# A decoder layer's recurrent scan on VectorE: outer product by heads, corrections by broadcast, fewer waits; with row groups in the LoRA matmuls and a new order in the product-key stage

## What is computed

```python
def step(state, rkv):
    r_t, k_t, v_t = rkv
    pred = jnp.einsum('bhij,bhj->bhi', state, k_t)
    err = pred - v_t
    state = dec * state - et * (err[..., :, None] * k_t[..., None, :])
    n = jnp.maximum(jnp.sqrt(jnp.sum(state * state, axis=(-2, -1), keepdims=True)), 1e-08)
    state = state * jnp.where(n > max_norm, max_norm / n, 1.0)
    wkv = jnp.einsum('bhij,bhj->bhi', state, r_t)
```

## Time and profile before

| | us |
|---|---|
| three runs, median (lowest to highest) | 6758.13 (6751.82 to 6759.17) |
| the profiled execution, its own time | 6756.8 |
| its span in the trace | 6755.0 |
| mean granted TensorE clock, share of full speed | 0.949 |
| PE busy in the span | 5962.8 |
| DVE busy | 5530.5 |
| ACT busy | 3576.0 |
| POOL busy | 3730.7 |

### The profile page before, as it was taken

The page is one execution under the profiler, slowest core; times in us unless marked ns, Lnnn a source line. Parts: engine busy times, 40 slices in busy tenths (PEclk is TensorE's granted clock), DMA queues, the critical chain, the costliest instruction groups (busy, mean ns, idle before and its releaser), DMA issues. The chain is left out here.

```text
span 6755.0 us, 179966 instructions
## 1 busy us (share of the span) xinstructions
PE 5962.8 (88%) x76324; PEld 4338.5 (64%) x76324; DVE 5530.5 (82%) x10471; ACT 3576.0 (53%) x8048; POOL 3730.7 (55%) x1761
## 2 busy tenths in 40 slices
PE   7566666799998899999999999999788789999999
PEld 5466665677777755555555555555566578888888
DVE  7798998555547879999999999999666588777886
ACT  5455554333333478888888888878355522222221
POOL 1576776111111169999999999999422122222232
PEclk9777777899999999999999999999899999999999
DMA  3232221111102331121112111111121100000000
GB/s 102 73 77 65 54 52 53 37 48 44 41 14 104 124 89 38 52 51 44 46 37 58 42 50 42 44 46 30 54 85 57 35 20 8 8 8 8 8 8 7
DMA packets 390641, 314.64 MB, mean 47 GB/s; under 512 B 171686, under 2 KB 358569, under 8 KB 389324
## 3 DMA queue, kind: packets, MB, share of 16 engines
q1 hardware_dynamic: 384150, 302.84, 15.4%
q10 hardware_dynamic: 5686, 0.29, 0.1%
HBM read 194.99 MB, written 108.01 MB: 45 GB/s over the span
## 5 line engine op out<-in xcount | busy, mean ns | idle before, releaser
L2386 POOL TENSOR_TENSOR ss_ch<-ss_h,ss_c_all 128x2048 f32<-128x2048 f32 x511 | 2325.6, 4622 | 33.9 <-DVE ss_h L2415 23.2
L2415 DVE TENSOR_TENSOR_SCAN ss_h<-ss_decay,banks 128x1024 f32<-128x1024 f32 x1024 | 2256.6, 2267 | 64.1 <-PE banks L2302 63.5
L2302 PE MATMUL banks<-ss_diag,ss_dxT 128*32 128x256 f32 x32768 | 1970.3, 381 | 25.8 <-DVE ss_h L2415 17.1
L2302 PEld LDWEIGHTS banks<-ss_diag,ss_dxT 128*32 128x32 f32 x32768 | 1008.0, 110 | 808.3 <-DVE ss_h L2415 196.1
L2366 ACT ACTIVATE ss_decay<-ss_dt,ss_neg_a 128x510 f32<-128x510 f32 x2048 | 1358.1, 710 | 257.5 <-DVE ss_h L2415 251.3
L2754 POOL TENSOR_TENSOR pk_blockhot<-pk_onehot,pk_parts 128x2048 bf16<-128x2048 bf16 x96 | 345.5, 3628 | 935.7 <-DVE pk_parts L2980 935.7
L2357 ACT ACTIVATE ss_diag<-ident,ss_bT 128x128 f32<-128x128 f32 x2016 | 685.2, 387 | 184.4 <-PE banks L2302 184.4
L812 PE MATMUL banks<-ms_rprod,ident 128*128 128x128 f32 x2048 | 465.4, 399 | 315.0 <-POOL ms_rprod L936 309.3
L2309 PE MATMUL banks<-ss_ch,ss_stacked 128*32 128x256 f32 x8192 | 635.5, 382 | 45.2 <-POOL ss_ch L2386 40.3
L812 PEld LDWEIGHTS banks<-ms_rprod,ident 128*128 128x128 f32 x2048 | 431.6, 258 | 342.5 <-POOL ms_rprod L936 278.3
L1045 POOL TENSOR_SCALAR l_ln_mv<-l_ln_mv 128x2 f32<-128x2 f32 x64 | 15.1, 236 | 985.0 <-DVE l_ln_mv L1040 985.0
(11 more groups left out here) (330 smaller groups left out, 9998.2 us busy)
## 6 DMA issues: line engine op xcount, KB each, us to landing
ss_dt<-keep_dt SPq DMA_DIRECT2D x256, 128.0 KB, 4.0
ss_c_all<-keep_cn SPq DMA_DIRECT2D x512, 64.0 KB, 2.1
keep_v<-ms_cx_values SPq DMA_DIRECT2D x32, 512.0 KB, 2.8
l_va<-keep_v SPq DMA_DIRECT2D x32, 512.0 KB, 4.4
l_kf<-keep_k SPq DMA_DIRECT2D x32, 256.0 KB, 2.8
keep_x<-l_x SPq DMA_DIRECT2D x32, 256.0 KB, 2.1
keep_xc<-si_xc SPq DMA_DIRECT2D x16, 512.0 KB, 3.5
keep_zs<-si_zs SPq DMA_DIRECT2D x16, 512.0 KB, 4.5
```

Source lines behind the costliest of these rows:

```text
L2302: m = T_.matmul(inp[u % 2][s * CB:(s + 1) * CB, g, :, t * P:(t + 1) * P], inputs[i % 2][0][:, g, t, u * CB:(u + 1) * CB], diag[slot][:, g, ...
L2386: G_.tensor_tensor(ch[u // 2 % 4][:, :, :, :, :].rearrange("p j g n t -> p j (g n t)"), h[u // 2 % 4][:, :, :, :, :].rearrange("p j g n t ...
L2415: V.tensor_tensor_scan(whole(h[u // 2 % 4][:, u % 2, :, :, :]), whole(decay[u % 4]), whole(inp[u % 2]), 0.0, ALU.mult, ALU.add).then_inc(s ...
```

## The change

There are four parts.

1. In the scan's step: `pull` stands before `ahead` instead of behind it; the two instructions that corrected one head each become one product for both heads with a broadcast factor and one difference for both heads; the factor's reciprocal counts on VectorE's own counter, which ScalarE waits on too, so the error's instruction waits on one semaphore instead of two; the outer product is made for each head by itself, the first as soon as the first head's error is there; ScalarE's two squares write buffers of their own, and the second no longer waits for the first.
2. In the chunk: `cut_chunk`, `measure` and `sum_gains` are split by heads, one piece to a step, and stand in front of the wait for the root instead of between error and outer product or behind the latter.
3. In the feed-forward of layer 0: the LoRA weights lie in two groups of 32 rows, for even and odd blocks, and the LoRA rows of the tokens are written twice; the two LoRA products of a pair of blocks are issued one behind the other, from two row groups into two banks, before the pair's first block. An even block waits until both banks are empty.
4. In `product_keys`: the second half of the scores is matched behind the last pair of gates instead of behind the second, and ScalarE makes the choosing tile's gates before it copies the scores.

```diff
-    square = sb("square", [P, D * D])
+    square = sb("square", [P, 2, D * D])
...
                 A.wait_ge(*(state if e else half).at(t))
-                A.activation(square[:, :], flat(S_[:, (t + 1) % 2, e, :, :]), ACT.Square, accum_out=n2[:, e:e + 1]
+                A.activation(square[:, e, :], flat(S_[:, (t + 1) % 2, e, :, :]), ACT.Square, accum_out=n2[:, e:e + 1]
                              ).then_inc(squared.sem, 1)
-                A.wait_ge(*squared.at(t, e + 1))
+            A.wait_ge(*squared.at(t))
             A.activation(root[:, :], n2[:, :], ACT.Sqrt).then_inc(rooted.sem, 1)
             if t + 1 < T:
-                A.wait_ge(*factored.at(t))
+                A.wait_ge(*factored[t + 1])
...
+    def cut_chunk(V, c, e):
         V.wait_ge(*summed_r.at((c + 1) * CH // GR - 1))
         if c > 1:
             V.wait_ge(*stored[c % 2].at(c // 2 - 1))
-        V.tensor_tensor(WKV[:, c % 2, :, :, :], bank[5 + c % 2][:, :].rearrange("p (t e d) -> p t e d", t=CH, e=2),
-                        rep(FF[:, c * CH + 1:(c + 1) * CH + 1, :], 3, D), ALU.mult).then_inc(cut.sem, 1)
...
+    def beside_root(V, c, u):
+        if c and u in (GR, GR + 1):
+            cut_chunk(V, c - 1, u - GR)
+        if c and u in (GR + 2, GR + 3):
+            measure(V, c - 1, u - GR - 2)
+        if c + 1 < CHUNKS and u in (CH - 2, CH - 1):
+            sum_gains(V, c + 1, u - CH + 2)
...
-        if t > 1:
-            V.wait_ge(*multiplied.at(t - 2))
-            V.tensor_reduce(ahead, kprod[t % 2][:, :, :, :], AX.X, ALU.add).then_inc(*own.up())
         if t:
             V.tensor_tensor(pull[:, :, :], err, rep(gain[:, t, :], 2, D), ALU.mult).then_inc(*own.up())
-            looked = own.now()
-            V.wait_ge(*looked)
-            correct(V, 0)
+            if t > 1:
+                V.wait_ge(*multiplied.at(t - 2))
+                V.tensor_reduce(ahead, kprod[t % 2][:, :, :, :], AX.X, ALU.add).then_inc(*own.up())
+            V.wait_ge(*own.now())
+            V.tensor_tensor(raw, ahead, rep(fdec[:, :], 2, D), ALU.mult).then_inc(*own.up())
+            decayed = own.now()
+            beside_root(V, c, u)
             V.wait_ge(*rooted.at(t - 1))
             V.tensor_scalar(inv, root[:, :], 1.0 / max_norm, 1.0, ALU.mult, ALU.max).then_inc(*own.up())
             clamped = own.now()
-            correct(V, 1)
-            corrected = own.now()
+            V.wait_ge(*decayed)
+            V.tensor_tensor(raw, raw, pull[:, :, :], ALU.subtract).then_inc(*own.up())
             V.wait_ge(*clamped)
-            V.reciprocal(FF[:, t, :], inv).then_inc(factored.sem, 1)
-            V.wait_ge(*corrected)
-            V.wait_ge(*factored.at(t - 1))
+            V.reciprocal(FF[:, t, :], inv).then_inc(*own.up())
+            factored[t] = own.now()
+            V.wait_ge(*factored[t])
+        erred = []
         for e in range(2):
             V.scalar_tensor_tensor(err[:, e, :], raw[:, e, :], FF[:, t, e:e + 1], VV[:, t, e, :], ALU.mult, ALU.subtract).then_inc(*own.up())
-        erred = own.now()
+            erred.append(own.now())
         if t == 0:
             V.tensor_tensor(fdec[:, :], FF[:, t, :], dec_held, ALU.mult).then_inc(*own.up())
-        if u == GR and c:
-            cut_chunk(V, c - 1)
-        V.wait_ge(*erred)
-        if u == GR + 1 and c:
-            measure(V, c - 1)
-        V.tensor_tensor(outer, rep(err, 3, D), rep(EK[:, t % (2 * CH), :, :], 2, D), ALU.mult).then_inc(*own.up())
-        if u == CH - 2 and c + 1 < CHUNKS:
-            sum_gains(V, c + 1)
-        V.wait_ge(*own.now())
+        grown = []
+        for e in range(2):
+            V.wait_ge(*erred[e])
+            V.tensor_tensor(outer[:, e, :, :], rep(err[:, e, :], 2, D), rep(EK[:, t % (2 * CH), e, :], 1, D), ALU.mult).then_inc(*own.up())
+            grown.append(own.now())
         if t > 1:
             V.wait_ge(*multiplied_r.at(t - 2))
         if t:
             V.wait_ge(*decays.at(t - 1))
         for e in range(2):
+            V.wait_ge(*grown[e])
             V.scalar_tensor_tensor(flat(after[:, e, :, :]), flat(now[:, e, :, :]), fdec[:, e:e + 1], flat(outer[:, e, :, :]),
                                    ALU.mult, ALU.subtract).then_inc((state if e else half).sem, 1)
...
         for f in range(FB):
-            fs = slice(f * P, (f + 1) * P)
-            if f > 1:
-                T_.wait_ge(*cut.at(b, f - 1))
-            project(T_, bank[F0 + f % 2], [wi[:, kt, fs] for kt in range(KC)] + [lb[:, fs]],
-                    [hT[:, kt, :] for kt in range(KC)] + [amT[:, :]]).then_inc(widened.sem, 1)
+            if f % 2 == 0:
+                if f:
+                    T_.wait_ge(*cut.at(b, f))
+                for n in range(2):
+                    of_pair = slice(n * E * R, (n + 1) * E * R)
+                    T_.matmul(bank[F0 + n][:, 0:T], lb[of_pair, f // 2 * P:(f // 2 + 1) * P], amT[of_pair, :], start=True, stop=False)
+            for kt in range(KC):
+                m = T_.matmul(bank[F0 + f % 2][:, 0:T], wi[:, kt, f * P:(f + 1) * P], hT[:, kt, :], start=False, stop=kt == KC - 1)
+            m.then_inc(widened.sem, 1)
             yield from nothing(2 if f < 6 else 1)
...
             for pair in range(PAIRS):
                 if apply is not None:
                     build(apply, pair)
-                if enter is not None and pair < 2:
-                    match(enter, pair)
+                if enter is not None and pair in (0, PAIRS - 1):
+                    match(enter, int(pair > 0))
...
+            if choose is not None:
+                gates(choose)
             if enter is not None:
                 take_scores(enter)
-            if choose is not None:
-                gates(choose)
```

More of the change, by code:

```diff
@@ L903, in vector, with measure @@
         m.then_inc(spread_ready.sem, 1)
-    def measure(V, c):
-        V.wait_ge(*cut.at(c))
-        for e in range(2):
-            V.bn_stats(moments[:, e, c * 6:(c + 1) * 6], WKV[:, c % 2, :, e, :]).then_inc(*own.up())
+    def measure(V, c, e):
+        V.wait_ge(*cut.at(c, e + 1))
+        V.bn_stats(moments[:, e, c * 6:(c + 1) * 6], WKV[:, c % 2, :, e, :]).then_inc(*own.up())
     def gpsimd(G):
@@ L948, in gpsimd @@
                 gains(n // CH + 1, GAIN.index(n % CH))
-    def cut_chunk(V, c):
+    def cut_chunk(V, c, e):
         V.wait_ge(*summed_r.at((c + 1) * CH // GR - 1))
```

38 lines of the change are left out of this document (21 added, 17 removed).

## The result

The changed kernel takes 6647.53 us (median of 4, 6643.99 to 6659.87) where the kernel before takes 6758.65 beside it: a ratio of 0.984, 95% interval 0.983 to 0.986, 111 us less. The forecast was 6634, in a range of 6610 to 6684. The profiled execution took 6643.99 (span 6642.2, mean granted clock 0.960).

| stretch | before | after | forecast |
|---|---|---|---|
| scan, first state to last | 919.4 | 829.8 | -91 |
| layer0_rest, first product of wkv to last l_mid | 869.3 | 865.8 | -10 |
| from there to the first state of ssm_scan | 387.1 | 381.8 | 0 |
| ssm_scan and layer1_attention | 2973.9 | 2970.7 | 0 |
| product_keys | 1356.5 | 1345.5 | -22 |

What follows compares the result with a forecast made beforehand. The prediction took VectorE's serial chain to bound the scan and TensorE to bound `layer0_rest`. The profiled 6756.8 us less 91 (scan), 10 (LoRA) and 22 (product keys) gave 6634, range 6610 to 6684.

Steps and rivals of the forecast that it cites:

- The walk: Scan step, instruction by instruction: 3.46 to 3.06 us, 101.6 in 254 steps, 91 after 4.6 and 6.4 given back.
- I price it and the difference at 0.18: Scan step on VectorE: the product for both heads and the difference each take 0.18 us, like `pull`.
- A half: Scan: one head's outer product on VectorE costs 0.41 to 0.42 us.
- The chunk's pieces: Scan: six split pieces cost 1.9 us a chunk instead of 1.6; 0.3 a chunk, 4.6 in all, given back.
- each of the four chunks waits 1.6 more: Scan's folding: steps get shorter but DMA transfers don't, so VectorE waits longer; 6.4 us given back.
- The rule of the Trainium skill: Rival, scan: only the number of chained instructions counts, waits are free; 6738 us, chance 0.03.
- The 0.07 of the sum: Scan step: the error starts 0.07 us earlier when it waits on one semaphore instead of two.
- The root's chain: Rival, scan: ScalarE's second square still waits, clamp 0.12 later, steps lose 0.10 to 0.12; 6659 us, chance 0.16.
- LoRA, -10 forecast: `layer0_rest`: paired row groups save 27.8 us, shape changes take 15.4, leaving 12; part becomes TensorE waits, so 10.
- My 0.24 for the changes of shape: `layer0_rest`: changing TensorE's array shape costs 0.24 us for each of 64 LoRA pairs, 15.4 in all.
- All 22 are saved: `product_keys`: the moved half match fills TensorE's wait for VectorE ahead of the up product, 22.2 us in 25 tiles.
- A rival's price: Rival: the change does nothing in the scan because GpSimd or TensorE paces it; 6750 us, chance 0.02.

Runs made afterwards that it cites:

- best: Changed kernel with the scan's sum ahead of `pull`, folding loads ahead of the context's stores, half the match before all gates, quarters behind pairs 2 and 4; 6620.6 us.
- outer_whole: Changed kernel with one outer product of 128x512 in place of the two halves; 6712.4 us.
- two_counters: Changed kernel with the reciprocal counting on a semaphore of its own again, so the error waits on two semaphores; 6664.1 us.
- lora_rows32: Kernel before with each LoRA product taking 32 rows of its operands instead of 128, at its old place, nothing side by side; 6789.5 us.
- only_lora: Kernel before with the LoRA row groups alone; 6748.5 us.
- best_apart: As `best`, with the first pair's gates half-way through the down products and the first half of the match behind those products; 6601.2 us.

## Why the prediction was right

The sum (-123) and the result (-111, of the span -113) differ by the product keys and by small sizes in the scan and in `layer0_rest`. The mechanisms of the scan and of the LoRA pair held; that of the product keys held for the wait and missed what the new order brought with it. Some of the agreement is luck, and it is named below.

- **Scan, -91 forecast, -89.6 measured.** The walk held place by place. Measured from `pull`'s start, with the forecast in brackets: product 0.82 (0.81), clamp 0.93 (0.91), error 1.35 (1.30), first half 1.64 (1.60), state 2.31 (2.26), next `pull` 3.09 (3.06). Mis-sized was "I price it and the difference at 0.18": both took 0.20, so VectorE, and not the root, sets the clamp, and 0.02 to 0.05 is lost. (The product and the difference for both heads at once, and `pull` ahead of the sum, were not tried alone.) The gain is 0.376 a step, 95.5 in 254, and not 101.6. A half took 0.422 (0.41 to 0.42). Given back was less than forecast. The chunk's pieces cost 0.18 more a chunk (51.17 less 16 quiet steps of 3.088 is 1.76, before 57.0 less 55.42 is 1.58), not 0.3: 2.8 and not 4.6. The folding's excess over a quiet chunk went from 9.7 in chunks 4 to 7 to 14.0: 4.3 and not 6.4, and not in equal shares. The clamp waited 4.01, 2.61 and 2.92 in chunks 5 to 7 and waits 3.17, 3.37, 2.71 and 4.13 in chunks 4 to 7; in chunk 5 it is less than before, where 5.6 was forecast. So "each of the four chunks waits 1.6 more" failed as it stands. The loads are late, as `best` shows, but by how much changes from chunk to chunk and kernel to kernel. In all, 95.5 less 2.8 and 4.3 is 88.4, and 89.6 was measured.
- **The waits, not the count.** The rule of the Trainium skill that I set against the rows ("VectorE: DVE Perf Modes", section "Rules for kernel authors") would have given 6738. `outer_whole` and `two_counters` decide it for this kernel. The reading that an instruction with two semaphores starts later was too simple: an event that comes last costs 0.035 where the instruction itself carries its wait, be it the only one or the first of three as in the state before, and 0.11 to 0.13 where the wait stands behind another and is carried ahead of the instruction. The 0.07 of the sum was right, because the change removed just such a wait.
- **The root's chain** was right in direction. The rival's price per step was right too (0.095), but in the whole kernel it is 15.6 and not 25, as the pieces hide it.
- **LoRA, -10 forecast, about -10 measured, half of it elsewhere, and that is luck.** `layer0_rest` lasted 864.4 to 868.9 in ten kernels with the pair (mean 866.6), 869.3 to 873.8 in three without (872.0): 5.4. The two products of a pair start 0.007 apart, as said. By the rows the pair saves 0.86 - 0.63 - 0.09 = 0.14 on TensorE, 9 in all (forecast 12). The other 4 did not turn into waits, as I had it: TensorE's waits of over 0.15 us in the stage are 99.8 to 102.4 in the ten kernels with the pair and 103.6 to 104.7 in the three without. Where they went is not shown. My 0.24 for the changes of shape is 0.29, as `lora_rows32` measures, and 64 x 0.43 is 27.5, not 27.8. The Trainium skill ("TensorEngine Tiling (Array Packing)", section "Key Properties") names the drain at a change of mode; these runs agree in that a change of shape costs time, and give its price. The other 5 us lie behind the stage, where I forecast nothing. Over 340 us there the granted clock is 0.96, and 0.94 before; a VectorE operation of the same line and shape takes 484 ns and took 488. It goes with the tile `lb`, as only it differs between `lora_rows32` and `only_lora` there besides the products. Whether its addresses or its load do it was not tried; the cause stays open.
- **Product keys, -22 forecast, -11 measured.** The step that failed is "All 22 are saved". The wait was saved (23 us), but the order that hides it makes one run of 288 small matmuls, and TensorE's instructions don't come fast enough for that: 26 more in gaps, a term that the sum had at nothing. What kept it from being a loss is a gain that I had not seen. In the kernel before 7 of 32 up products run partly at the lower clock; this one, behind a gap and the wait, took 16.99 where the others take 14.08, and over it the granted clock (third from the end of the window's row) is 0.81, between its levels of 2.4 and 1.2 GHz:

```profile
5833.85 0.76 PE L2812 MATMUL banks<-pk_blockhot,pk_rowhot 64*128 64x32 bf16 x40 [1.65 <-issue]
5834.54 0.56 PE L2789 MATMUL banks<-ident,pk_vals 64*64 64x64 f32 x12
5835.99 16.99 PE L2823 MATMUL banks<-pk_up,pk_act 128*128 128x256 f32 x64 [0.89 <-DVE pk_act L2994]
```
```profile
5835.00:5853.00 18.00, 17.11 (x70) 14.47 (x67) 17.35 (x48) 0.00 (x0) 11.54 (x5) 0.81 0.00 1
```

In the changed kernel this happens once. The seven cost 13 us (1.4 to 2.9 each), and the changed kernel's one 1.7, so -23 + 26 - 11 = -8, of the 11. That the part came out as a gain at all is luck: the wait and the gaps alone come to a loss of 3. By the means of six and four kernels (1343.8 and 1359.2) the order is worth 15, not 11. The four kernels with the old order have 6 to 10 such products, the ten with a new one 0 to 2.
- **A rival's price.** If the change had done nothing in the scan, the 32 us elsewhere would still have been gained: 6725, and not 6750. No run bears on it, as the scan did gain.

## What to carry to other kernels

Walk a serial step with three sizes from the trace: an instruction that waits for nothing starts ahead of its forerunner's end, one that waits for it starts behind, one whose last event is not the wait that the instruction itself carries later still; then put independent work between producer and consumer, and see that the event that comes last has a wait to itself or the one that stands first. Before moving work to fill a wait, list what the moved work itself hid (here a gelu) and how many small instructions the new order puts in a row, since they have to be brought to the engine too. A change of the array's shape is paid for each excursion, so few long excursions beat many short ones, as far as the supply of instructions allows.

## What the runs showed that I had not expected

**TensorE runs out of instructions.** In `product_keys` 288 gates are 576 instructions with their weight loads. They took 4.4 us while fed. The page of the changed kernel has 76324 matmuls and as many weight loads, and 9.83 MB in 600 packets of the instruction queue q8, 16 KB each. With its 1090 other instructions that is one packet for every 256 of TensorE's. Transfers over the 16 us of the tile shown above, in slices of 0.4 us, and their queue (packets, MB, share):

```profile
GB/s 0 0 0 0 0 41 0 0 0 0 0 0 0 0 41 0 0 0 0 0 0 0 0 0 0 41 0 0 0 0 0 0 0 0 0 20 41 0 0 0
...
q8 instruction: 4, 0.07, 1.8%
```

Packets start at 6002.3, 6006.0, 6010.1 and 6014.5, every 4 us, while 576 small instructions need 2.3 of them in 4.4. The gap lasts from 6011.1 to 6012.6, and the packet of 6010.1 ends at 6011.2.

That the supply is the cause can be read from where the gaps stand. Number all of TensorE's instructions in a trace in order of time, weight loads and event-semaphore instructions too: all 36 gaps of the changed kernel stand at the same place within 256 (number 193 to 195), and so do all 373 gaps of the 14 kernels. Each ends 1.2 to 1.6 us (median 1.4) behind the end of a packet. So the gaps lie whole packets of instructions apart, whatever the program has there, and end soon after a packet has come. Which of these places cost a gap depends on the order: 39.1 to 44.0 us with 96 and 288 in a row, 44.6 with 192 and 192, 16.6 to 18.2 with 96, 96 and 192, 12.8 with four times 96 or with 96 apart, 96 and 192. No single rule of mine fits all of them, the 17.7 of `best_apart` among them; what decides the length of a gap stays open.

**A wait of 0.9 us can cost more than itself.** In the kernel before, 28 of the 32 up products stood behind a wait of 0.9 or more, and 7 of them then ran partly at the lower granted clock, for up to 2.9 us more. That the wait brings it on is argued from the counts (6 to 10 such products with the old order, 0 to 2 with a new one); why it happens in some tiles and not in others stays open.
